# Softplus straight into the transfers' source, the router's chain as nine operations in SBUF, and a new order on every engine

## What is computed

```python
uo = layernorm(x) @ W_in.T;  u, o = split(uo)
u = silu(causal_conv(u) + conv_b)
delta_lo, b, c = split(u @ W_gate.T)
delta = softplus(delta_lo @ W_delta.T + delta_bias)
h = exp(A * delta) * h + (delta * u) * b        # over time, 256 channels x 16 states
y = (sum_states(h * c) + D * u) * sigmoid(o) * o
x = x + y @ W_out.T
scores = softmax(layernorm(x) @ gate_w.T);  w, i = top_k(scores, 2);  w = w / sum(w) * 2.5
x = x + sum_e combine[e] * mlp_e(layernorm(x)) + mlp_shared(layernorm(x))
```

## Time and profile before

| | |
|---|---|
| runs, median (lowest to highest) | 1155.44 us (1155.27 to 1155.64) |
| the profiled execution | 1155.91 us, its span 1154.1 us |
| busy, share of the span | PE 93%, DVE 91%, ACT 93%, POOL 91% |
| mean granted TensorE clock | 0.97 of full speed |

### The profile page before, as it was taken

The page is one execution under the profiler, slowest core; times in us unless marked ns, Lnnn a source line. Parts: engine busy times, 40 slices in busy tenths (PEclk is TensorE's granted clock), DMA queues, the critical chain, the costliest instruction groups (busy, mean ns, idle before and its releaser), DMA issues.

```text
span 1154.1 us, 25028 instructions
## 1 busy us (share of the span) xinstructions
PE 1069.2 (93%) x8947; PEld 906.1 (79%) x8947; DVE 1051.9 (91%) x1510; ACT 1070.0 (93%) x2177; POOL 1047.6 (91%) x374
## 2 busy tenths in 40 slices
PE   4658999999999999999999999999999999998897
PEld 4436788888888888888888888888888888886786
DVE  4467999999999999999999999999999999999953
ACT  5779999999999999999999999999999999999852
POOL 3699899999999999999999999999999999999810
PEclk9567999999999999999999999999999999999999
DMA  7444444433444443334444433344444333443000
GB/s 187 110 104 112 98 121 109 105 90 89 114 116 103 121 102 106 90 94 111 120 104 121 102 100 86 103 112 110 113 121 102 92 89 104 112 99 96 6 6 10
DMA packets 71478, 115.01 MB, mean 100 GB/s; under 512 B 8173, under 2 KB 30394, under 8 KB 71354
## 3 DMA queue, kind: packets, MB, share of 16 engines
q1 hardware_dynamic: 71354, 113.42, 38.3%
HBM read 41.04 MB, written 5.24 MB: 40 GB/s over the span
## 4 chain that ended last, share of the span: by engine, by line
ACT 53%; PE 28%; issue 12%; DVE 4%; SPq 1%; DMA 1%; POOL 1%; ACTq 0%; DVEq 0%; POOLq 0%
ACT decay_ps L529 20%; PE work_ps L1023 8%; ACT g_silu L516 7%; PE work_ps L1106 6%; PE work_ps L1115 4%; PE acc_ps L1067 4%; ACT L644 3%; ACT L636 3%; ACT L678 3%; ACT L629 3%; PE acc_ps L1143 3%; ACT L697 3%; DVE features L771 2%; ACT xn L550 2%; ACT work_ps L608 2%
## 5 line engine op out<-in xcount | busy, mean ns | idle before, releaser
L437 POOL TENSOR_TENSOR inject<-rep,bc 128x2048 f32<-128x2048 f32 x128 | 581.4, 4566 | 6.2 <-DMA rep<-dd 6.2
L451 POOL TENSOR_TENSOR read<-state,bc 128x1024 f32<-128x1024 f32 x192 | 457.8, 2394 | 25.6 <-DVE state L749 22.0
L749 DVE TENSOR_TENSOR_SCAN state<-decay_ps,inject 128x1024 f32<-128x1024 f32 x192 | 438.2, 2283 | 13.5 <-ACT decay_ps L529 13.5
L529 ACT ACTIVATE decay_ps<-rep,neg_a 128x255 f32<-128x255 f32 x1024 | 426.5, 465 | 3.9 <-DVE decay_ps L764 2.2
L1143 PE MATMUL acc_ps<-ffn_down,features 128*128 128x128 f32 (+1 forms) x1792 | 235.8, 275 | 2.0 <-DVE features L779 2.0
L1143 PEld LDWEIGHTS acc_ps<-ffn_down,features 128*128 128x128 f32 (+1 forms) x1792 | 220.8, 191 | 4.9 <-DVE features L779 2.6
L1115 PE MATMUL work_ps<-xn2T_part,ffn_up 128*128 128x256 f32 x1344 | 203.6, 291 | 10.9 <-ACT g_silu L516 9.6
L1106 PEld LDWEIGHTS work_ps<-xn2T_part,ffn_gate 128*128 128x128 f32 x1344 | 171.4, 190 | 45.4 <-issue 24.7
L1106 PE MATMUL work_ps<-xn2T_part,ffn_gate 128*128 128x256 f32 x1344 | 199.8, 293 | 5.5 <-DVE features L771 5.5
L1115 PEld LDWEIGHTS work_ps<-xn2T_part,ffn_up 128*128 128x128 f32 x1344 | 173.0, 190 | 34.8 <-ACT g_silu L516 24.1
L771 DVE TENSOR_TENSOR features<-g_silu,work_ps 128x512 f32<-128x512 f32 x224 | 152.6, 681 | 25.1 <-PE work_ps L1115 22.7
(11 more groups left out here) (136 smaller groups left out, 1244.3 us busy)
## 6 DMA issues: line engine op xcount, KB each, us to landing
rep<-dd SPq DMA_DIRECT2D x256, 256.0 KB, 4.8
bc<-bc_rows SPq DMA_DIRECT2D x64, 512.0 KB, 3.9
x_in<-in_L_attn_x_dram SPq DMA_DIRECT2D x32, 128.0 KB, 2.2
out_dram<-result SPq DMA_DIRECT2D x32, 128.0 KB, 1.9
bc_rows<-g_sb SPq DMA_DIRECT2D x32, 32.0 KB
state<-in_L_ffn_w_gate_dram SPq DMA_DIRECT2D x1, 704.0 KB, 4.4
inject<-in_L_ffn_w_up_dram SPq DMA_DIRECT2D x1, 704.0 KB, 5.9
ffn_down<-in_L_ffn_w_down_dram SPq DMA_DIRECT2D x1, 704.0 KB, 7.4
```

The costliest lines, as they stand in the source:

```text
L437: pool.tensor_tensor(inject[:, slot:slot + many], du_all, b_all, ALU.mult).then_inc(inject_done, many)
L451: pool.tensor_tensor(read[:, slot:slot + many], state[:, first:first + many], c_all, ALU.mult).then_inc(read_done, many)
L529: last = act.activation(decay_ps[:, at % 2, j, 1:T], rep[(HALVES * n + half) % RP][:, j, 0, 1:T], ACT.Exp, scale=neg_a[:, col:col + 1])
L749: dve.tensor_tensor_scan(to, decays, inject[:, at % RI].rearrange("p j t -> p (j t)"), 0.0, ALU.mult, ALU.add).then_inc(state_done, 1)
```

## The change

Three edits of substance and a new order.

`softplus` writes into `dd[:, :, 0, :]` and `copy_delta` is gone; `times_u` takes delta from there. `marked`, `inverse` and `comb` become SBUF tensors, and `route` is cut into `mark_best`, `pick_scores`, `sum_scores`, `invert_sum`, `combine` and `comb_high`, which with `top_logit`, `shift_logits` and `comb_low` stand as nine operations apart. The transfer of c is issued in a function of its own. The PSUM banks are dealt out anew, and the lists of ACT, DVE and PE are in another order.

```diff
             def softplus(n):
                 act.wait_ge(z_copied, n)
-                act.activation(delta_ps, z_sb[:], ACT.Softplus).then_inc(delta_done, 1)
-
-            def copy_delta(n):
-                act.wait_ge(delta_done, n + 1)
                 for half in range(HALVES):
                     act.wait_ge(rep_in[half], 16 * JB * n)
-                act.copy(dd[:, :, 0, :], delta_ps).then_inc(dd_done, 1)
+                act.activation(dd[:, :, 0, :], z_sb[:], ACT.Softplus).then_inc(dd_done, 1)
...
-                dve.tensor_tensor(dd[:, :, 1, :], delta_ps, u[n % RU][:], ALU.mult).then_inc(du_done, 1)
+                dve.tensor_tensor(dd[:, :, 1, :], dd[:, :, 0, :], u[n % RU][:], ALU.mult).then_inc(du_done, 1)
...
-            def route(f):
+            def mark_best(f):
                 dve.wait_ge(best_done, TILES * (f + 1))
                 for j in range(TILES):
-                    dve.match_replace(out=marked_ps[:, j, :], in_to_replace=best[:, j, :], in_values=shifted[:, j, :],
+                    dve.match_replace(out=marked[:, j, :], in_to_replace=best[:, j, :], in_values=shifted[:, j, :],
                                       imm_value=1.0).then_inc(marked_done, 1)
+
+            def pick_scores(f):
                 dve.wait_ge(marked_done, TILES * (f + 1))
                 dve.wait_ge(expd_done, 2 * f + 1)
-                dve.scalar_tensor_tensor(out=picked, in0=marked_ps[:, :, FILL:], scalar=1.0, in1=expd[:],
-                                         op0=ALU.is_equal, op1=ALU.mult).then_inc(comb_steps, 1)
+                dve.scalar_tensor_tensor(out=picked, in0=marked[:, :, FILL:], scalar=1.0, in1=expd[:],
+                                         op0=ALU.is_equal, op1=ALU.mult).then_inc(picked_done, 1)
...
-                dve.reciprocal(inv_ps, denom[:]).then_inc(comb_steps, 1)
+            def invert_sum(f):
+                dve.wait_ge(denom_done, f + 1)
+                dve.reciprocal(inverse[:], denom[:]).then_inc(inverse_done, 1)
+
+            def combine(f):
+                dve.wait_ge(inverse_done, f + 1)
+                dve.scalar_tensor_tensor(out=comb[:], in0=picked, scalar=SCALE,
+                                         in1=inverse[:].unsqueeze(2).broadcast_to([P, TILES, EXPERTS]), op0=ALU.mult,
+                                         op1=ALU.mult).then_inc(comb_done, 1)
+
+            def comb_high(f):
+                dve.wait_ge(comb_done, f + 1)
                 dve.wait_ge(combT_mm, f)
-                dve.tensor_copy(comb_parts[:, :, 0:EXPERTS], comb_ps).then_inc(comb_split, 1)
+                dve.tensor_copy(comb_parts[:, :, 0:EXPERTS], comb[:]).then_inc(comb_split, 1)
 
             def comb_low(f):
                 dve.wait_ge(comb_split, 2 * f + 1)
-                dve.tensor_tensor(comb_parts[:, :, LOW:LOW + EXPERTS], comb_ps, comb_parts[:, :, 0:EXPERTS].bitcast(F32),
+                dve.tensor_tensor(comb_parts[:, :, LOW:LOW + EXPERTS], comb[:], comb_parts[:, :, 0:EXPERTS].bitcast(F32),
                                   ALU.subtract).then_inc(comb_split, 1)
...
-            def spread_bc(n):
+            def spread_b(n):
                 sp.wait_ge(bc_out, 16 * (n + 1))
                 sp.wait_ge(inject_done, count(GROUPS * (n - 1)))
                 spread_rows(n, 0, b_in)
+
+            def spread_c(n):
                 sp.wait_ge(read_done, count(OTHERS * (n - 1)))
                 sp.wait_ge(read_own_done, count(len(OWN) * (n - 1)))
                 spread_rows(n, 1, c_in)
```

More of the change, by code:

```diff
@@ L392, in body @@
             def body(k, on, later):
+                if later(1):
+                    spread_c(k + 1)
                 if on(-3):
@@ L461, in body @@
                     inject_group(0, 2, 2)
+                if on(-1):
+                    read_group(k - 1, 7)
                 if later(0):
@@ L636, in body @@
                     act.preload_act_table_set("softplus")
[L637 to L641, removed]
                     softplus(k + 1)
+                if later(2):
+                    xn_high(k + 2)
                 if on(0) or later(3) or on(-1):
@@ L873, in body @@
                 if on(0):
+                    read_own_group(k, 0)
+                if on(-3):
+                    weigh(k - 3, 5)
+                if on(0):
+                    clear_first(k, 0)
                     scan(k, 1)
+                if on(-3):
+                    add_result(k - 3)
                 if on(-2):
-                    best_eight(k - 2)
+                    pick_scores(k - 2)
+                if on(-1):
+                    add_x1(k - 1)
+                if on(-2):
+                    sum_scores(k - 2)
+                if on(-1):
+                    stats_x1(k - 1)
+                if later(1):
+                    times_u(k + 1)
                 if on(0):
-                    read_own_group(k, 0)
-                    clear_first(k, 0)
+                    scan(k, 2)
                 if on(-2):
                     gated_up(k - 2, 2)
-                if on(-3):
-                    add_result(k - 3)
-                if on(-1):
-                    add_x1(k - 1)
-                    stats_x1(k - 1)
-                if on(0):
-                    scan(k, 2)
-                if later(1):
-                    times_u(k + 1)
-                if on(-2):
                     gated_up(k - 2, 3)
+                    invert_sum(k - 2)
                 if on(0):
                     scan(k, 3)
+                if on(-2):
+                    combine(k - 2)
+                    comb_high(k - 2)
+                    gated_up(k - 2, 4)
+                    comb_low(k - 2)
+                if on(0):
                     scan(k, 4)
                 if on(-2):
-                    gated_up(k - 2, 4)
+                    gated_up(k - 2, 5)
+                if on(0):
+                    read_own_group(k, 4)
+                    take_y(k, 0)
+                    clear_first(k, 4)
+                if on(-2):
+                    gated_up(k - 2, 6)
+                if on(0):
+                    scan(k, 5)
+                if on(-1):
+                    top_logit(k - 1)
+                    shift_logits(k - 1)
+                if on(-2):
+                    weigh(k - 2, 0)
+                    weigh(k - 2, 1)
+                    weigh(k - 2, 2)
+                if on(0):
+                    scan(k, 6)
+                    scan(k, 7)
+                if on(-1):
+                    gated_up(k - 1, 0)
                 if later(4):
@@ L1166, in body @@
                 if on(-3):
-                    down(k - 3, 7)
                     down(k - 3, 8)
                     down(k - 3, 9)
+                if on(-2):
+                    pe.wait_ge(silu_done, PAIRS * (k - 2) + 4)
+                if later(2):
+                    turn_xn(k + 2)
+                if on(-3):
                     down(k - 3, 10)
```

256 lines of the change are left out of this document (108 added, 148 removed).

## The result

The changed kernel takes 1398.95 us (median; 1390.42 to 1404.28) against 1155.36 for the kernel before, a ratio of 1.2114 (1.2076 to 1.2152). The profiled execution has a span of 1388.7 us against 1154.1, 234.6 more. It is the shortest of the four runs; the others go up to 1404.28 us with the mean granted clock, 0.930 in the shortest, 0.922 in the next and 0.914 to 0.915 in the two longest.

A forecast was written before the change was run, and what follows sets the result against it. It took ACT as the bound, three engines within 2%. DVE's waits behind POOL made the step 41.1 us instead of 33.1; 8.0 over 31 steps, 248 us on 1155.9, gave 1404, said as 1400 us; 8-in-10 range 1225 to 1540.

The forecast's parts named there:

- POOL's floor: POOL's own work in a steady step, 32.5 us, claimed as the least step length for any order.
- the prediction's last part: Signs to check: if the suspected DVE rows keep their old lengths, the pace is POOL's and the time 1143 us.
- What is taken away: Per step: ACT loses a 0.48 us copy, to about 32.7; DVE's spread routing chain saves about 0.6, to about 32.2.
- the drain: On ACT, log of variances and reciprocal root now stand adjacent, exposing about 0.1 us a step (an estimate).
- The step by these terms: Steady step from the savings alone, without any DVE waiting behind POOL: 32.6 or 32.8 us.
- The fast case: DVE never waits behind POOL: step 32.7 us, time 1143 us, 1.1% faster; chance of ending faster 0.12.
- The step I had to judge: Two-SBUF-input DVE instruction issued behind POOL's: between no wait and the rest of POOL's instruction each time, the second was taken.
- The prediction's two rows: Set-up rows: POOL's inject stood still behind two-input L866 (0.44 us excess); DVE's two SBUF-to-SBUF L962 waited for POOL's memset (1.33 us).
- The walk: One steady step from scan 3's end: waits 9.2 plus DVE's work 32.2 gave 41.4 us; walked through, 41.1, which was taken.
- Only some held: Rival: comb_high isn't held or slips in, comb_low waits only to 2.4; step 36.6 us, time 1264 us; chance 0.26.
- POOL keeps the way: Rival: held DVE instructions pass only when POOL waits for a scan; step about 47 us, time 1587 us; chance 0.12.
- Never held: Rival: only POOL waits behind DVE, never the reverse; step 32.7 us, time 1143 us; chance 0.17, of which 0.12 faster.

The follow-up runs named there:

- e1: Changed kernel with times_u, pick_scores, combine, comb_high and comb_low as one-input reductions over a length-one axis, their arithmetic left out: 1135.01 us, ratio 0.9835.
- e3: Kernel before with one edit: times_u reads delta from dd in SBUF instead of PSUM, the ACT copy stays: 1192.74 us, ratio 1.0329.
- e9: Kernel before with the delta part alone: softplus writes dd, ACT's copy is gone, times_u has two SBUF inputs; old order and router: 1190.48 us, ratio 1.0311.
- e6: Changed kernel with POOL's injects issued one group at a time instead of two, DVE's list unchanged: 1315.75 us, ratio 1.1408.
- e2: Changed kernel with comb_high alone written as a one-input reduction over a length-one axis, same result: 1239.26 us, ratio 1.0742.
- e7: Changed kernel with PE's transposes of xn2 repeated eight times, same result, to fill PE's gap: 1379.90 us, ratio 1.1975.
- e5: Changed kernel with the four routing operations as one-input reductions, so times_u alone has two SBUF inputs: 1177.09 us, ratio 1.0191.
- e4: Kernel before with the router's marks, inverse and combined weights in SBUF, its order and delta unchanged: 1422.08 us, ratio 1.2319.

## Why the prediction was right

**What bounds the kernel.** ACT with the least to spare, POOL and the others close behind: right. With all holds gone e1 stops at 32.72 us, where ACT waits for nothing. POOL's floor was not reached: it waits 0.34 us a step there, so its own work is 32.4. The pace there is ACT's; the prediction's last part put it down to POOL.

**What is taken away.** ACT's busy time in a step is 32.36 us in e1, where it was 32.71: 0.35 less, near the 0.48 for the copy less the 0.1 for the drain. Between e3 and e9, which differ in the copy and in what `softplus` writes, it is 0.44. (The page's total for the changed kernel, 1069.8, doesn't show it: instructions that overlapped now stand apart, and the same list that is busy for 32.37 us in a step of e1 is busy for 32.79 in one of the changed kernel.) The step by these terms was 32.7, and e1's is 32.72. The fast case was put at 1143, and e1 measured 1135: of the 20.1 us by which its profiled span is shorter than that of the kernel before, 10.7 lie in 28 steady steps and 7.9 ahead of the first `combine`, which the prediction did not look at. e9 shows that the saving is worth nothing in the steady step once DVE is held.

**DVE behind POOL with two SBUF inputs.** The step I had to judge. Right, and shown by e3 (one operand moved), e1 (all removed) and e6 (the length follows POOL's instruction). The rule cited from the Trainium skill (SBUF — State Buffer, "Who interferes with whom") agrees with these runs in the direction that the trace before didn't show, and in the length of 571 of 587 holds (more on the other 16 below). It says that copies and casts can enter a two-port mode, not that each does; in e2 and the changed kernel the cast of 128x16 from SBUF to SBUF behaves so, and the cast to `comb_parts` from PSUM, before, took 0.17 us beside an inject of POOL's. The prediction's two rows are not quite one case either: the page asks for a GpSimd instruction that reads SBUF where DVE has two SBUF inputs, and L962 with one input was held by a memset, which only writes. Whether the two-input kind would wait for a POOL instruction that only writes, no run here shows: all of POOL's in a steady step read SBUF.

**The walk.** Term by term, from the step at 601.16:

| | predicted | measured, own time taken off |
|---|---|---|
| `comb_high` | 2.3 | 2.37 - 0.17 = 2.2 |
| `comb_low` | 3.8 | 4.00 - 0.17 = 3.8 |
| `pick_scores` | 1.6 | 1.62 - 0.17 = 1.45 |
| `times_u` | 1.5 | 2.14 - 0.67 = 1.5 |
| step | 41.1 | 40.42 |

The holds sum to 8.95 us instead of 9.2. DVE's own work is therefore 40.42 - 8.95 = 31.5 us, where I had 32.2; whether the waits or the gain of spreading the chain were taken too small, no run tells apart. Together with what the walk had already dropped, the step is 0.68 us under the 41.1 that I took, which is worth 21 us too much over 31 steps. The other error has the opposite sign: eight steps lengthened by 17.8 us in all, which e7 ties to PE's gaps. I had said that PE with 32.4 us of work fits, and had not asked what the new gaps do to its clock. 7.31 us over 29 steps is 212 us, and with 17.8 it makes 230 of the 234.6 us that the span grew. So 1400 against 1399 is closer than the terms deserve: two errors of some 20 us with opposite signs, and a median that lies 8.5 us above the profiled run. That is luck; what was right is the mechanism and its size.

**The rivals.** Only some held: not so here, but e2 is that case and its walk gave 36.6 against 36.1. POOL keeps the way: refuted as a rule by `pick_scores`, which ends at 605.30, at the border between an inject and a read that needed no wait, and by e6. But it happens: in 16 of the 587 holds (executions more than 0.2 us above the shortest of their line) in the profiles of the changed kernel and of e2 to e7 and e9 (six in e2, five in e5, three in e4, one each in e6 and e7, none in the changed kernel) DVE misses the border and is held through the next instruction too. The prediction had it as all or nothing. Never held: refuted by e3.

## What to carry to other kernels

When POOL works all the time on SBUF, look at each DVE instruction beside it for a second SBUF input or an SBUF-to-SBUF copy; its length in the profile then follows POOL's instructions, 4.0 us for 16 columns in a steady step here and 8.4 us at worst (e4), and a PSUM operand, even at the price of a copy on another engine, can be the cheaper form. Where two SBUF operands must meet, one tensor that holds both and a reduction over the pair reads them as one input, for 0.56 us more at 512 columns than with one operand in PSUM. And in such a kernel the order of DVE's list against POOL's, and the length of POOL's instructions, decide which operation is held and for how long, so a new order is to be walked against POOL's list before its savings are counted.

## What the runs showed that I had not expected

- At the borders between two of POOL's instructions DVE mostly got in first, also with POOL's next one ready (`comb_low` between two injects of one pair, in the changed kernel and in e6), but not always: see e2, e4 and e5. What decides it is open; in e2 the same operation both gets in and misses at the same border in different steps.
- What counts is not how many SBUF tensors a row names. `MATCH_REPLACE8` names two, `best` and `shifted`, in both kernels (the text on the kernel before passes over it), and takes 0.15 to 0.17 us in every step, as at 598.78 in the changed kernel, inside the injects of 596.18 to 605.26.
- POOL's 4-column shift, 0.21 us before, takes 0.66 us behind a `times_u` that began its columns first (607.56), and 0.65 in e3.
- Softplus writes 630 ns into SBUF where it took 602 into PSUM (31 executions each), 28 ns that the saving of the copy gives back.
- Repeating transposes eight times, work for nothing, made the changed kernel about 19 us faster; the granted clock of 400 to 700 us rose from 0.95 to 0.97.
